# Two attention loops of a two-layer transformer kernel: handing the exponentials on in parts instead of all together

## The chip, the cores and the metric

The kernel runs on all 8 cores of one Trainium2 chip. Every core runs the same program on its own batch element (2048 tokens of width 1024), and the cores do not exchange data. The metric is the device time of one launch on the slowest core, in microseconds.

## What is computed

The reference has two layers. Layer 0 adds, to the input x, a differential attention (16 query heads, 4 key/value heads, causal, two softmaxes over half heads of 32) and a feed-forward part whose operands are quantised to FP4 in blocks of 16. Layer 1 adds a linear attention and a stack of two local-attention blocks with a GELU MLP each. The change touches the two softmax attentions only:

```python
# layer 0, differential attention: 16 heads, two score sets each, T = 2048
s1 = jnp.einsum('bhqd,bhkd->bhqk', q1, k1) * scale      # half heads, 32 wide
s2 = jnp.einsum('bhqd,bhkd->bhqk', q2, k2) * scale
a1 = jax.nn.softmax(jnp.where(causal, neg_inf, s1), axis=-1)
a2 = jax.nn.softmax(jnp.where(causal, neg_inf, s2), axis=-1)
y  = jnp.einsum('bhqk,bhkd->bhqd', a1 - lam * a2, v)     # then RMS norm, @ Wout.T

# layer 1, local attention, twice (DEPTH = 2): 8 heads of 64, window 512
sim  = jnp.einsum('bhwid,bhwjd->bhwij', bq, bk)          # each window sees itself and the one before
sim  = jnp.where(mask, -jnp.finfo(sim.dtype).max, sim)   # i < j, or i > j + 512
attn = jax.nn.softmax(sim, axis=-1)
out  = jnp.einsum('bhwij,bhwjd->bhwid', attn, bv)
```

## The kernel before

The program is written engine by engine. `te`, `ve`, `se`, `ge` and `sy` are TensorE, VectorE, ScalarE, GpSimd and SyncE, and each engine runs its own instructions in the order of the code. They meet in a few counting semaphores: `k.s_mm` is raised by TensorE, `k.s_v` by VectorE, `k.s_s` by ScalarE. `sem.inc(instr)` raises the count when that instruction is done, `sem.wait(engine)` makes an engine wait until everything raised so far in the code has arrived. `se.drain()` and `ve.drain()` wait until their engine is empty, and are often what carries the raise. The stages run one after the other, with barriers between them. PSUM is held as two tiles of four banks, `psA` and `psB`, each [128, 4, 512] in float32, and nearly all of SBUF as one tile, ARENA.

**Layer 0, `emit_l0_scores`.** For each of 8 pairs of heads (`qt`) and each of 4 blocks of 512 queries (`c`) the loop over `kt` goes through 4c+4 blocks of 128 keys. That is 8 x (4+8+12+16) = 320 iterations. In the last four of each block (`masked`) the causal diagonal runs through the tile and only columns `off` to 512 are computed, so that the width is 512, 384, 256 or 128: 128 iterations, 32 of each width. The other 192 have the width 512. One iteration:

1. TensorE makes four score tiles, `psA[:, jj]` for jj = 0 to 3, each with a bias matmul of one row (L703) and the score matmul of 32 rows (L706).
2. ScalarE waits for all four and takes four exponentials into `UT[:, jj]` (L714), then a drain, which raises `s_s` (L715).
3. If masked, VectorE multiplies the diagonal block of all four by the 0/1 mask `M01`, in one instruction of 4 x 128 columns (L720).
4. TensorE waits for that and adds four matmuls of values (V) with `UT[:, jj]` into `psB[0:65, jj]` (L729). The row 65 is the sum of the exponentials.

The next iteration's scores need `psA` to be read out (a wait on `s_s`) and stand behind the four value matmuls in TensorE's order.

**Layer 1, `emit_l1f_attn`, once for each of two blocks.** For 4 pairs of heads (`t4`), 4 windows (`w`) and 4 blocks of 128 queries (`lq`) there are 64 iterations per block, 128 in all. A query block sees `nblk` key blocks, five in 48 of the 64 iterations (640 columns), and one to four in the others. One iteration:

1. TensorE makes negated scores of both heads (jj = 0, 1), each in two banks of `psA` (L1453, L1457).
2. VectorE takes the minimum along each row, for head 0 and then head 1, into `NM` (L1466), and drains (L1467).
3. ScalarE takes both exponentials with the minima as bias into `UT[:, jj]` (L1471), and drains (L1473).
4. TensorE transposes the 2 x nblk blocks one by one through two banks of `psB` (L1483), and VectorE copies each out, those on the diagonal times a mask (L1487, L1489, L1491). From the third on, a transpose waits for the copy two before it.

After each window come the value matmuls (L1500), a few small steps and the next window.

Of the kernel before, what the change touches and what calls it, by code (L numbers as in the profile page):

```python
# [11 lines left out]
AF = mybir.ActivationFunctionType  # L12
ALU = mybir.AluOpType
AX = mybir.AxisListType
# [577 lines left out]
def emit_l0_scores(k, h, Q, K2, VT, out_h):  # L592
    nc = k.nc
    te, ve, se, ge, sy = k.te, k.ve, k.se, k.ge, k.sy
# [6 lines left out]
    UT = ar.bf(4, 512)  # L601
# [33 lines left out]
    for kt2 in range(2):  # L635
# [4 lines left out]
        for cc in range(4):  # L640
            k.s_mm.inc(te.matmul(k.psB[:, cc, :], P4t[:], SQB[:, 512 * cc:512 * cc + 512],
                                 start=True, stop=True))
# [16 lines left out]
    for kv in range(4):  # L659
        for g4 in range(4):  # L660
            off = 128 * (kv % 2) + kv // 2 + 64 * (g4 % 2)
# [6 lines left out]
    M01 = k.M01  # L668
# [3 lines left out]
    for qt in range(8):  # L672
        kvv = qt // 2
# [5 lines left out]
        for cc in range(4):  # L679
            k.s_mm.inc(te.matmul(k.psB[:, cc, :], P4t[:], SQB[:, 512 * cc:512 * cc + 512],  # L680
                                 start=True, stop=True))
# [12 lines left out]
        for c in range(4):  # L694
            nkt = 4 * c + 4
            k.s_v.wait(te)
            for kt in range(nkt):
                masked = kt >= 4 * c
                off = 128 * (kt - 4 * c) if masked else 0
                w = 512 - off  # L700
                te.wait_ge(k.s_s.h, k.s_s.n)
                for jj in range(4):
                    te.matmul(k.psA[:, jj, off:512], ones1b[32 * jj:32 * jj + 1, 0:128],  # L703
                              BT[32 * jj:32 * jj + 1, 512 * c + off:512 * c + 512],
                              start=True, stop=False, tile_position=(32 * jj, 0))
                    mm = te.matmul(k.psA[:, jj, off:512],  # L706
                                   KARR[32 * jj:32 * jj + 32, kvv, 128 * kt:128 * kt + 128],
                                   Q[32 * jj:32 * jj + 32, qt, 512 * c + off:512 * c + 512],
                                   start=False, stop=True, tile_position=(32 * jj, 0))
                    k.s_mm.inc(mm)  # L710
                k.s_mm.wait(se)
                k.s_v.wait(se)
                for jj in range(4):
                    se.activation(UT[:, jj, off:512], k.psA[:, jj, off:512], AF.Exp)  # L714
                k.s_s.inc(se.drain())  # L715
                if masked:
                    k.s_s.wait(ve)
                    uview = UT[:, :, off:off + 128]
                    m01b = M01[:].unsqueeze(1).broadcast_to((128, 4, 128))
                    k.s_v.inc(ve.tensor_tensor(uview, uview, m01b, op=ALU.mult))  # L720
                if DEV_TAP == "ut" and qt == 0 and c == 3 and kt == 0:
                    full_barrier(k)
                    dump_fm(k, UT.rearrange("p a b -> p (a b)").unsqueeze(1), k.out_h, 1)
                    return
                k.s_s.wait(te)
                if masked:
                    k.s_v.wait(te)
                for jj in range(4):
                    k.s_mm.inc(te.matmul(k.psB[0:65, jj, off:512], VT[:, kt, kvv, 0:65],  # L729
                                         UT[:, jj, off:512], start=(kt == 0), stop=(kt == nkt - 1)))  # L730
            k.s_mm.wait(ve)
            for jj in range(4):
                ve.tensor_copy(OE[0:65, jj, :], k.psB[0:65, jj, :])
# [42 lines left out]
            if DEV_TAP == "rc" and qt == 0 and c == 0:  # L776
# [8 lines left out]
                             axis=AX.X, op=ALU.add)  # L785
# [58 lines left out]
    for j in range(NT):  # L844
        k.s_st.wait(ve)
        for oc in range(2):
            pb = k.psB[:, 2 * (j % 2) + oc, :]
            te.wait_ge(k.s_v.h, max(0, k.s_v.n - 3))
            for ft in range(8):
                mm = te.matmul(pb, Q[:, ft, 128 * j:128 * j + 128],  # L850
                               WOB[:, ft, 512 * oc:512 * oc + 512],
                               start=(ft == 0), stop=(ft == 7))
# [437 lines left out]
def emit_l1f_attn(k, h, out_h, XINT, l, CQ, SQ, CK, SK,  # L1290
                  P64R, M01L, PHB, E2B, E2Q, E2K, QSR):
    te, ve, se, ge, sy = k.te, k.ve, k.se, k.ge, k.sy
    ar = k.ar
    M01 = k.M01
# [32 lines left out]
    for oc in range(12):  # L1327
        b = oc % 2
# [3 lines left out]
        for tc in range(4):  # L1332
            pb = k.psA[:, tc % 4, :]
            te.wait_ge(k.s_s.h, max(0, k.s_s.n - 3))
            for ic in range(8):
# [3 lines left out]
                               start=(ic == 0), stop=(ic == 7))  # L1339
# [13 lines left out]
    UT = ar.bf(2, 640)  # L1353
# [85 lines left out]
    NM = k.stats[:, 44:46]  # L1439
    for t4 in range(4):  # L1440
        for w in range(4):
            for lq in range(4):
                qc = 4 * w + lq
                kts = list(range(max(0, qc - 4), qc + 1))
                nblk = len(kts)
                wcols = 128 * nblk
                te.wait_ge(k.s_s.h, k.s_s.n)
                te.wait_ge(k.s_v.h, k.s_v.n)
                for jj in range(2):
                    lhs = QKVB[64 * jj:64 * jj + 64, t4, 128 * qc:128 * qc + 128]  # L1450
                    kbase = 128 * kts[0]
                    w0 = min(512, wcols)
                    mm = te.matmul(k.psA[:, 2 * jj, 0:w0], lhs,  # L1453
                                   QKVB[64 * jj:64 * jj + 64, 4 + t4, kbase:kbase + w0],
                                   start=True, stop=True, tile_position=(64 * jj, 0))
                    if wcols > 512:
                        mm = te.matmul(k.psA[:, 2 * jj + 1, 0:wcols - 512], lhs,  # L1457
                                       QKVB[64 * jj:64 * jj + 64, 4 + t4,
                                            kbase + 512:kbase + wcols],
                                       start=True, stop=True, tile_position=(64 * jj, 0))  # L1460
                    k.s_mm.inc(mm)
                k.s_mm.wait(ve)
                ve.wait_ge(k.s_s.h, k.s_s.n)
                for jj in range(2):
                    flat = k.psA[:, 2 * jj:2 * jj + 2, :].rearrange("p a b -> p (a b)")
                    ve.tensor_reduce(NM[:, jj:jj + 1], flat[:, 0:wcols], axis=AX.X, op=ALU.min)  # L1466
                k.s_v.inc(ve.drain())  # L1467
                k.s_v.wait(se)
                for jj in range(2):
                    flat = k.psA[:, 2 * jj:2 * jj + 2, :].rearrange("p a b -> p (a b)")  # L1470
                    se.activation(UT[:, jj, 0:wcols], flat[:, 0:wcols], AF.Exp,  # L1471
                                  bias=NM[:, jj:jj + 1], scale=-1.0)
                k.s_s.inc(se.drain())  # L1473
                k.s_s.wait(te)
                vb2 = k.s_v.n
                i2 = 0
                for jj in range(2):
                    for b, kt in enumerate(kts):
                        ktr = kt - 4 * w + 4
                        if i2 >= 2:  # L1480
                            te.wait_ge(k.s_v.h, vb2 + i2 - 1)
                        pvb = k.psB[:, 2 + i2 % 2, :].bitcast(BF16)[:, 0:128]
                        k.s_mm.inc(te.transpose(pvb, UT[:, jj, 128 * b:128 * b + 128], k.idb[:]))  # L1483
                        k.s_mm.wait(ve)
                        dst = UTT[:, jj, ktr, 128 * lq:128 * lq + 128]
                        if b == 0 and qc >= 4:
                            k.s_v.inc(ve.tensor_tensor(dst, pvb, M01L[:], op=ALU.mult))  # L1487
                        elif b == nblk - 1:
                            k.s_v.inc(ve.tensor_tensor(dst, pvb, M01[:], op=ALU.mult))  # L1489
                        else:  # L1490
                            k.s_v.inc(ve.tensor_copy(dst, pvb))  # L1491
                        i2 += 1
            te.wait_ge(k.s_v.h, k.s_v.n)
            ktrs = [3, 4, 0, 1, 2, 5, 6, 7] if w > 0 else [4, 5, 6, 7]
            for jj in range(2):
                for idx, ktr in enumerate(ktrs):
                    kt = ktr + 4 * w - 4
# [393 lines left out]
```

## Time and profile before

| | us |
|---|---|
| time before, median of 2 runs | 11788.0 (11786.84 to 11789.16) |
| the profiled execution's own time | 11779.26 |
| its span on the slowest core (core 6) | 11777.7 |
| spans of the eight cores | 11709.6 to 11777.7 |
| busy: TensorE, VectorE, ScalarE, GpSimd | 4204.9, 3347.4, 1550.8, 1078.3 |

No engine is busy for more than 36% of the span. The page of the profile lists what each engine did; the views that follow it are the totals by line, the timeline (each row is a start time, a duration, the engine, the line, the operation, the tiles and their shapes, and in brackets how long the engine had been idle and who released it), and sums over stretches of time. The profile's times are those of one execution.

### The profile page before, as it was taken

How to read it: one execution, taken by the hardware profiler on the slowest of the kernel's cores; microseconds unless marked ns; L12 is line 12 of the kernel's file. 1: busy time of each engine (PE TensorE's matmuls, PEld its weight loads, DVE VectorE, ACT ScalarE, POOL GpSimd, SP SyncE). 2: the span in 40 equal slices, each digit the busy share in tenths (PEclk: the TensorE clock that was granted, in tenths of full speed). 3: DMA queues.
4: the chain of work that ended last, by engine and by line, in shares of the span. 5: the costliest groups of instructions: out<-in, count | busy, mean ns of one | idle time of the engine just before them, and what ended most of it. 6: DMA issues, size and time to landing. Idle time of an engine off the chain costs nothing.

```text
span 11777.7 us, 65862 instructions; the slowest of 8 cores (11709.6 to 11777.7 us)
## 1 busy us (share of the span) xinstructions
PE 4204.9 (36%) x17922; PEld 1690.8 (14%) x18113; DVE 3347.4 (28%) x7665; ACT 1550.8 (13%) x2754; POOL 1078.3 (9%) x737
## 2 busy tenths in 40 slices
PE   0000033434444433333434233344436234244353
PEld 0000011111111111111212111111112011111111
DVE  6555542111112133233325545001003544201000
ACT  1000013333333200000111111100001111100000
POOL 1222210000000011111000000111110000111110
PEclk9999985555555667766666555677767555676666
DMA  1111110000000101111310001332331001232323
GB/s 54 34 43 43 44 28 0 1 0 0 0 0 0 62 29 47 54 31 52 93 59 10 0 1 23 34 29 22 31 36 12 0 1 22 27 29 22 36 28 70
DMA packets 563009, 326.39 MB, mean 28 GB/s; under 512 B 466694, under 2 KB 519046, under 8 KB 561628
## 3 DMA queue, kind: packets, MB, share of 16 engines
q0 software_dynamic: 406448, 125.85, 10.4%
q1 hardware_dynamic: 156212, 196.32, 5.1%
q8 instruction: 167, 2.74, 0.1%
q14 instruction: 182, 1.49, 0.0%
HBM read 388.63 MB, written 50.92 MB: 37 GB/s over the span
## 4 chain that ended last, share of the span: by engine, by line
PE 33%; DVE 20%; DMA 15%; POOL 7%; ACTq 6%; issue 6%; ACT 6%; DVEq 5%; SPq 1%; POOLq 0%; PEldq 0%
PE psA L1744 8%; DMA ARENA<-w 7%; PE psB L729 4%; ACTq L715 4%; PE psB L1772 3%; POOL qC L291 2%; POOL ARENA L317 2%; DVE qB L1399 2%; PE psA L937 2%; DMA ARENA<-wquT_s 2%; POOL ARENA L1757 2%; DMA ARENA<-x_s 2%; ACT ARENA L714 1%; PE psB L1483 1%; PE psA L940 1%
## 5 line engine op out<-in xcount | busy, mean ns | idle before, releaser
L1744 PE MATMUL psA<-ARENA 128*128 128x512 bf16 (+1 forms) x2760 | 982.1, 530 | 1624.6 <-DMA ARENA<-w 1617.0
L333 PE MATMUL psA<-c_idb,ARENA 128*128 128x128 bf16 x888 | 146.2, 257 | 2248.6 <-POOL ARENA L317 1923.0
L1778 DVE TENSOR_TENSOR ARENA<-ARENA,psB 128x512 bf16<-128x512 bf16 x64 | 41.1, 683 | 2950.2 <-PE psB L1772 2950.2
L729 PE MATMUL psB<-ARENA 128*65 128x512 bf16 (+3 forms) x1280 | 522.1, 562 | 824.5 <-ACTq L715 509.2
L714 ACT ACTIVATE ARENA<-psA 128x512 bf16<-128x512 f32 (+3 forms) x1280 | 578.8, 539 | 919.7 <-PE psA L706 919.3
L1744 PEld LDWEIGHTS psA<-ARENA 128*128 128x128 bf16 (+1 forms) x2816 | 347.8, 128 | 2259.3 <-issue 2184.5
L720 DVE TENSOR_TENSOR ARENA<-ARENA,c_m 128x512 bf16<-128x512 bf16 x128 | 54.4, 425 | 1553.0 <-ACTq L715 1553.0
L291 POOL TENSOR_TENSOR qC<-qC,qA 128x2048 f32<-128x2048 f32 (+2 forms) x70 | 284.3, 4061 | 1959.0 <-DVEq L289 1959.0
L1751 ACT ACTIVATE qC<-psA,B1GC 128x512 bf16<-128x512 f32 (+1 forms) x176 | 120.9, 687 | 2500.4 <-PE psA L1744 2500.3
L1483 PE MATMUL psB<-c_idb,ARENA 128*128 128x128 bf16 x1120 | 229.4, 270 | 564.4 <-ACTq L1473 414.3
L333 PEld LDWEIGHTS psA<-c_idb,ARENA 128*128 128x128 bf16 x888 | 91.2, 103 | 2294.4 <-issue 2272.0
L1757 POOL TENSOR_TENSOR ARENA<-qC 128x512 bf16<-128x512 bf16 (+1 forms) x176 | 201.2, 1143 | 2243.4 <-ACTq L1755 2243.4
L1772 PE MATMUL psB<-ARENA 128*128 128x512 bf16 (+1 forms) x1376 | 356.0, 412 | 3.3 <-issue 1.7
L729 PEld LDWEIGHTS psB<-ARENA 128*65 128x65 bf16 x1280 | 170.4, 161 | 1185.8 <-issue 1174.6
L937 PE MATMUL psA<-ARENA 128*128 128x512 bf16 (+1 forms) x745 | 202.1, 419 | 382.6 <-DMA ARENA<-wquT_s 268.6
L1471 ACT ACTIVATE ARENA<-psA,stats 128x640 bf16<-128x640 f32 (+4 forms) x256 | 172.1, 723 | 1048.8 <-DVEq L1467 1048.8
L317 POOL TENSOR_TENSOR ARENA<-qC,qbm 128x2048 bf16<-128x2048 bf16 (+2 forms) x70 | 230.4, 3291 | 602.5 <-DVEq L311 602.5
L947 DVE TENSOR_TENSOR ARENA<-ARENA,psA 128x512 f32<-128x512 f32 (+1 forms) x96 | 61.7, 643 | 701.3 <-ACT ARENA L944 701.3
L944 ACT ACTIVATE ARENA<-psA 128x512 f32<-128x512 f32 (+1 forms) x96 | 53.9, 561 | 1479.7 <-PE psA L940 1479.7
L293 DVE SCALAR_TENSOR_TENSOR qA<-qC,qB 128x2048 f32<-128x2048 f32 (+2 forms) x70 | 145.5, 2078 | 304.4 <-POOL qC L291 304.4
L335 DVE COPY ARENA<-psA 128x128 bf16<-128x128 bf16 x888 | 139.0, 215 | 288.2 <-PE psA L333 283.9
L275 DVE TENSOR_REDUCE qbm<-ARENA 128x128 f32<-128x2048 f32 (+2 forms) x70 | 145.1, 2073 | 255.1 <-DMA ARENA<-wu 84.7
(343 smaller groups left out, 6970.5 us busy)
## 6 DMA issues: line engine op xcount, KB each, us to landing
ARENA<-w POOLq DMA_DIRECT2D x336, 256.0 KB, 4.8
ARENA<-x_s SPq DMA_DIRECT2D x80, 512.0 KB, 3.4
x_s<-ARENA SPq DMA_DIRECT2D x48, 512.0 KB
ARENA<-wqgT_s SPq DMA_DIRECT2D x20, 1024.0 KB, 5.9
ARENA<-wquT_s SPq DMA_DIRECT2D x20, 1024.0 KB, 8.4
ARENA<-x_in SPq DMA_DIRECT2D x32, 512.0 KB, 3.7
ARENA<-wg SPq DMA_DIRECT2D x11, 1024.0 KB, 6.2
ARENA<-wu SPq DMA_DIRECT2D x11, 1024.0 KB, 6.3
```

The lines of the kernel that those rows point to most:

```text
L291: k.s_g.inc(g.tensor_tensor(C[:, 0:W], C[:, 0:W], A[:, 0:W], op=ALU.add))
L317: k.s_g.inc(g.tensor_tensor(Q3, psi3, bm12b, op=ALU.mult))
L333: k.s_mm.inc(k.te.transpose(pv, src, identity))
L714: se.activation(UT[:, jj, off:512], k.psA[:, jj, off:512], AF.Exp)
L715: k.s_s.inc(se.drain())
L729: k.s_mm.inc(te.matmul(k.psB[0:65, jj, off:512], VT[:, kt, kvv, 0:65], UT[:, jj, off:512], start=(kt == 0), stop=(kt == nkt - 1)))
L937: te.matmul(k.psA[:, 0, 0:ocw], XQF[:, ic, 128 * j:128 * j + 128], WGS[:, ic, 0:ocw], start=(ic == 0), stop=(ic == 7))
L1399: ve.reciprocal(NRM[:], NRM[:])
L1483: k.s_mm.inc(te.transpose(pvb, UT[:, jj, 128 * b:128 * b + 128], k.idb[:]))
L1744: mm = te.matmul(k.psA[0:ocw, ag, :], W1S[:, ag, b, ic, 0:ocw], XHh[:, ic, toff:toff + 512], start=(ic == 0), stop=(ic == 7))
L1757: k.s_g.inc(ge.tensor_tensor(AHq[0:ocw, hc, :], AT[0:ocw, :], GH[0:ocw, :], op=ALU.mult))
L1772: mm = te.matmul(pb, AHq[0:kcw, hc, 128 * tch:128 * tch + 128], W2R[0:kcw, hc, 512 * dc:512 * dc + 512], start=False, stop=(hc == 21))
```

## The change

In layer 0 the four exponentials are dealt with in two halves. After the second exponential `s_s` is raised by the activation itself, and not by a drain; VectorE masks these two (2 x 128 columns), TensorE does the value matmuls of these two, and then the same happens with the third and fourth. All eight instructions of ScalarE and TensorE are still there, VectorE has two smaller mask multiplications instead of one, and the one drain is gone.

In layer 1 the minimum of head 0 raises `s_v` itself, and the exponential of head 0 waits for that one only; likewise for head 1. Each exponential raises `s_s`, and the transposes of head jj wait for the exponential of head jj only (`ecnt[jj]`). Both drains are gone. No tile and no buffer changes in either loop.

```diff
--- before.py
+++ after.py
@@ -710,24 +710,27 @@
                     k.s_mm.inc(mm)
                 k.s_mm.wait(se)
                 k.s_v.wait(se)
-                for jj in range(4):
-                    se.activation(UT[:, jj, off:512], k.psA[:, jj, off:512], AF.Exp)
-                k.s_s.inc(se.drain())
-                if masked:
-                    k.s_s.wait(ve)
-                    uview = UT[:, :, off:off + 128]
-                    m01b = M01[:].unsqueeze(1).broadcast_to((128, 4, 128))
-                    k.s_v.inc(ve.tensor_tensor(uview, uview, m01b, op=ALU.mult))
+                m01b2 = M01[:].unsqueeze(1).broadcast_to((128, 2, 128))
+                for half in range(2):
+                    jjs = (0, 1) if half == 0 else (2, 3)
+                    se.activation(UT[:, jjs[0], off:512], k.psA[:, jjs[0], off:512], AF.Exp)
+                    k.s_s.inc(se.activation(UT[:, jjs[1], off:512],
+                                            k.psA[:, jjs[1], off:512], AF.Exp))
+                    if masked:
+                        k.s_s.wait(ve)
+                        uview = UT[:, jjs[0]:jjs[0] + 2, off:off + 128]
+                        k.s_v.inc(ve.tensor_tensor(uview, uview, m01b2, op=ALU.mult))
+                    k.s_s.wait(te)
+                    if masked:
+                        k.s_v.wait(te)
+                    for jj in jjs:
+                        k.s_mm.inc(te.matmul(k.psB[0:65, jj, off:512], VT[:, kt, kvv, 0:65],
+                                             UT[:, jj, off:512],
+                                             start=(kt == 0), stop=(kt == nkt - 1)))
                 if DEV_TAP == "ut" and qt == 0 and c == 3 and kt == 0:
                     full_barrier(k)
                     dump_fm(k, UT.rearrange("p a b -> p (a b)").unsqueeze(1), k.out_h, 1)
                     return
-                k.s_s.wait(te)
-                if masked:
-                    k.s_v.wait(te)
-                for jj in range(4):
-                    k.s_mm.inc(te.matmul(k.psB[0:65, jj, off:512], VT[:, kt, kvv, 0:65],
-                                         UT[:, jj, off:512], start=(kt == 0), stop=(kt == nkt - 1)))
             k.s_mm.wait(ve)
             for jj in range(4):
                 ve.tensor_copy(OE[0:65, jj, :], k.psB[0:65, jj, :])
@@ -1461,20 +1464,20 @@
                     k.s_mm.inc(mm)
                 k.s_mm.wait(ve)
                 ve.wait_ge(k.s_s.h, k.s_s.n)
+                ecnt = []
                 for jj in range(2):
                     flat = k.psA[:, 2 * jj:2 * jj + 2, :].rearrange("p a b -> p (a b)")
-                    ve.tensor_reduce(NM[:, jj:jj + 1], flat[:, 0:wcols], axis=AX.X, op=ALU.min)
-                k.s_v.inc(ve.drain())
-                k.s_v.wait(se)
-                for jj in range(2):
-                    flat = k.psA[:, 2 * jj:2 * jj + 2, :].rearrange("p a b -> p (a b)")
-                    se.activation(UT[:, jj, 0:wcols], flat[:, 0:wcols], AF.Exp,
-                                  bias=NM[:, jj:jj + 1], scale=-1.0)
-                k.s_s.inc(se.drain())
-                k.s_s.wait(te)
+                    k.s_v.inc(ve.tensor_reduce(NM[:, jj:jj + 1], flat[:, 0:wcols],
+                                               axis=AX.X, op=ALU.min))
+                    se.wait_ge(k.s_v.h, k.s_v.n)
+                    flat2 = k.psA[:, 2 * jj:2 * jj + 2, :].rearrange("p a b -> p (a b)")
+                    k.s_s.inc(se.activation(UT[:, jj, 0:wcols], flat2[:, 0:wcols], AF.Exp,
+                                            bias=NM[:, jj:jj + 1], scale=-1.0))
+                    ecnt.append(k.s_s.n)
                 vb2 = k.s_v.n
                 i2 = 0
                 for jj in range(2):
+                    te.wait_ge(k.s_s.h, ecnt[jj])
                     for b, kt in enumerate(kts):
                         ktr = kt - 4 * w + 4
                         if i2 >= 2:
```

## Rows read from the trace of the kernel before

**Rows 1.** Sums over stretches: layer 0 loop, part of it, projections, layer 1 loop.

```profile
core 6: us, PE busy (x) PEld busy (x) DVE busy (x) ACT busy (x) POOL busy (x), PEclk, DMA share, GB/s
1827.00:3990.00 2163.00, 896.89 (x4481) 277.77 (x4488) 382.28 (x1315) 713.42 (x1440) 0.00 (x0) 0.50 0.00 0
2000.00:2050.00 50.00, 27.47 (x118) 6.37 (x116) 0.00 (x0) 18.58 (x36) 0.00 (x0) 0.50 0.00 0
1650.00:1700.00 50.00, 49.74 (x228) 22.65 (x232) 0.00 (x0) 17.24 (x30) 0.00 (x0) 1.00 0.00 0
6585.00:7210.00 625.00, 240.03 (x1194) 111.42 (x1194) 259.91 (x971) 87.33 (x129) 0.00 (x0) 0.53 0.00 1
```

**Rows 2.** Timeline, layer 0, one iteration without mask.

```profile
2504.16 2.06 ACT L714 ACTIVATE ARENA<-psA 128x512 bf16<-128x512 f32 x4 [3.30 <-PE psA L706]
...
2506.39 1.89 PE L729 MATMUL psB<-ARENA 128*65 128x512 bf16 x4 [2.49 <-ACTq L715]
...
2508.21 0.62 PE L703 MATMUL psA<-ARENA,c_ones1b 1*128 1x512 bf16 x4
2509.51 2.06 ACT L714 ACTIVATE ARENA<-psA 128x512 bf16<-128x512 f32 x4 [3.30 <-PE psA L706]
```

**Rows 3.** Timeline, layer 0, the end of that iteration and the four masked widths.

```profile
2510.49 1.09 ACT L714 ACTIVATE ARENA<-psA 128x512 bf16<-128x512 f32 x2
2511.70 0.42 DVE L720 TENSOR_TENSOR ARENA<-ARENA,c_m 128x512 bf16<-128x512 bf16 x1 [47.91 <-ACTq L715]
...
2512.28 1.89 PE L729 MATMUL psB<-ARENA 128*65 128x512 bf16 x4 [3.02 <-DVE ARENA L720]
...
2515.20 1.64 ACT L714 ACTIVATE ARENA<-psA 128x384 bf16<-128x384 f32 x4 [3.62 <-PE psA L706]
...
2517.53 1.46 PE L729 MATMUL psB<-ARENA 128*65 128x384 bf16 x4 [2.59 <-DVE ARENA L720]
...
2520.08 1.21 ACT L714 ACTIVATE ARENA<-psA 128x256 bf16<-128x256 f32 x4 [3.25 <-PE psA L706]
...
2521.99 1.03 PE L729 MATMUL psB<-ARENA 128*65 128x256 bf16 x4 [2.44 <-DVE ARENA L720]
...
2523.62 0.79 ACT L714 ACTIVATE ARENA<-psA 128x128 bf16<-128x128 f32 x4 [2.33 <-PE psA L706]
...
2525.10 0.61 PE L729 MATMUL psB<-ARENA 128*65 128x128 bf16 x4 [1.74 <-DVE ARENA L720]
```

**Rows 4.** Totals by line and shape: exponentials, minima, and two rows to compare with.

```profile
L714 ACT ACTIVATE ARENA<-psA 128x512 bf16<-128x512 f32 x896 | 462.5, 603 | 634.0 <-PE psA L706 633.6
...
L1466 DVE TENSOR_REDUCE stats<-psA 128x1 f32<-128x640 f32 x192 | 149.3, 819 | 102.3 <-PE psA L1457 102.3
...
L1471 ACT ACTIVATE ARENA<-psA,stats 128x640 bf16<-128x640 f32 x192 | 141.9, 789 | 868.9 <-DVEq L1467 868.9
...
L1342 ACT ACTIVATE ARENA<-psA 128x512 bf16<-128x512 f32 x96 | 57.3, 597 | 210.6 <-PE psA L1337 210.6
...
L307 DVE TENSOR_TENSOR qC<-qC,qA 128x1024 bf16<-128x1024 bf16 x20 | 13.8, 692 | 1.5
```

**Rows 5.** Timeline, layer 1, one iteration of five key blocks.

```profile
6656.87 1.56 DVE L1466 TENSOR_REDUCE stats<-psA 128x1 f32<-128x640 f32 x2 [1.08 <-PE psA L1457]
6658.55 1.48 ACT L1471 ACTIVATE ARENA<-psA,stats 128x640 bf16<-128x640 f32 x2 [16.34 <-DVEq L1467]
...
6660.19 0.37 PE L1483 MATMUL psB<-c_idb,ARENA 128*128 128x128 bf16 x2 [3.51 <-ACTq L1473]
6660.56 0.23 DVE L1487 TENSOR_TENSOR ARENA<-psB,M01L 128x128 bf16<-128x128 bf16 x1 [2.14 <-PE psB L1483]
6660.70 0.21 DVE L1491 COPY ARENA<-psB 128x128 bf16<-128x128 bf16 x1
6660.90 0.23 PEld L1483 LDWEIGHTS psB<-c_idb,ARENA 128*128 128x128 bf16 x2 [0.60 <-issue]
...
6661.65 0.24 PEld L1483 LDWEIGHTS psB<-c_idb,ARENA 128*128 128x128 bf16 x2 [0.51 <-issue]
```

## Prediction

> **What bounds the kernel now.** I read the sums over stretches first. Layer 0's attention loop takes 2163 us, and in it TensorE is busy for 897 us, ScalarE for 713 and VectorE for 382, with no DMA traffic at all [rows 1]. The loop of layer 1 takes 625 us for one of its two blocks, with 240, 87 and 260 us [rows 1]. No engine is full in either: they take turns. So I went to the timeline, where the reader is to see that each engine's work begins just after the end of another's.
>
> An iteration of layer 0 without mask: four exponentials from 2504.16 to 2506.22, 0.17 us later four value matmuls at 2506.39, scores at 2508.21, the next exponentials at 2509.51, and so 5.35 us in all. While ScalarE works TensorE is idle ("2.49 <-ACTq L715"), and while TensorE works ScalarE is ("3.30 <-PE psA L706") [rows 2]. With a mask 0.12 us of handing over, 0.42 us of VectorE and 0.16 us of handing over come between the exponentials and the value matmuls [rows 3].
>
> An iteration of layer 1 with five key blocks: two minima from 6656.87 to 6658.43, 0.12 us later two exponentials to 6660.03, 0.16 us later the first transpose. From there on transposes and copies go in pairs at 0.75 us a pair (6660.90 to 6661.65) [rows 5].
>
> Everything that one of these chains loses comes off the span one to one, as the stages are serial and no DMA waits in them.
>
> **Layer 0, no mask (192 iterations).** The second exponential ends 1.09 us after the first began, the fourth 2.06 us [rows 3, 2]. After the change value matmuls 0 and 1 can start 0.17 us after the end of the second, while ScalarE goes on. What does a value matmul cost in a stream? The totals of four fall by 0.43 us for every 128 columns less (1.89, 1.46, 1.03, 0.61 [rows 3]), which is 0.107 us per matmul and 128 columns: 0.43, 0.32, 0.21 and 0.11 us for the four widths. Likewise the exponentials: 2.06, 1.64, 1.21, 0.79 fall by 0.42 per 128 columns for four, and the third one starts 0.98 us after the first (2509.51 to 2510.49), so 0.49 each at 512 columns [rows 2, 3]. Two matmuls take 0.86 us, exponentials 2 and 3 take 0.97 us: the first half of the matmuls is hidden with 0.1 us to spare. Matmuls 2 and 3 then begin where all four begin today, and the next scores come 2 x 0.43 = 0.86 us earlier. 192 x 0.86 = **165 us**. Cover gone, this is zero.
>
> **Layer 0, mask (128 iterations, 32 of each width).** Two matmuls fewer on the path: 2 x (0.43 + 0.32 + 0.21 + 0.11) = 2.14 us, times 32 = 68 us. They are hidden here too, since at each width two exponentials take longer than two matmuls (at 128 columns 2 x 0.17 against 2 x 0.11). And the mask is cut in two, of which only the second is on the path. No row shows 2 x 128 columns. 512 columns took 0.42 us, 1024 in the same types 0.69 us [rows 3, 4]: 0.27 per 512, so 0.16 fixed, and 0.29 us for 256. That is 0.13 x 128 = 17 us gained. At worst the half costs as much as the whole, and the gain is 0. Sum with mask **85 us**.
>
> The fixed part is where a rule speaks against the change. The Trainium skill (VectorE: DVE Perf Modes, section on the TRN2 errata) says that each VectorE instruction on SBUF pays a fixed price between instructions, so that small tiles pay it again and again. By its figures (58 cycles and one for every two columns, at 0.96 GHz) the half would be an estimated 0.19 us and the whole 0.33, where the trace has 0.42; the difference of 0.13 us is the same, and so is the sum. The doubled fixed part lies beside the other half's exponentials.
>
> **Layer 1 (128 iterations).** Today the first transpose comes 3.32 us after the first minimum began. After: minimum 0 (0.82 us [rows 4]) + 0.12 + exponential 0 (0.79 [rows 4]) + 0.16 = 1.89 us, so 1.43 us earlier. Is anything late next? Minimum 1 ends 1.56 us after the start, +0.12 exponential 1 may begin at 1.73, when ScalarE is free, and ends at about 2.5; +0.16, head 1 can be transposed from 2.7. Head 0's five transposes last until 1.89 + 5 x 0.375 = 3.8, so this wait is covered. 96 iterations have 640 columns: 96 x 1.43 = 137 us. The other 32 have 128 to 512, half as many on average, and I scale the gain by columns: 32 x 0.72 = 23 us. **160 us** in both blocks.
>
> **The waits as such.** Raising a semaphore in mid-stream must be quick, and must not part instructions that overlap. For VectorE the trace shows both: the copy of 6660.56 ends at 6660.79, TensorE goes on at 6660.90 while the next copy, begun at 6660.70, still runs [rows 5]. For ScalarE there is no such row. Bounds: nothing, or each iteration loses the overlap of consecutive exponentials, 0.60 - 0.49 = 0.11 us [rows 4], once: 320 x 0.11 = 36 us. I take nothing, for the likeness to VectorE's row. The drains that go may give a little back: behind a drain TensorE came 0.17 us after ScalarE's last work, behind VectorE's raise 0.11 us (6660.79 to 6660.90 [rows 5], the weight load, with the matmul 0.03 us after it). 448 hand-overs x 0.03 = 13 us: not counted, but in the range.
>
> **Sum.** 165 + 85 + 160 = 410 us off. On the profiled execution's own 11779.3 this is 11369; it stands 9 us below the median of the runs, 11788.0, which gives **11378 us**, 3.5% faster.
>
> **Rivals.**
>
> *Handed on late.* ScalarE's raise from the second exponential shows only when its queue is empty. Then layer 0's halves give nothing, and layer 1's, where ScalarE has one exponential at a time between waits, stay: 11788 - 160 = 11628 us, within 2%. For it: no row of ScalarE. Against it: VectorE's row above.
>
> *The clock rises.* In the loop of layer 0 TensorE has its granted clock at 0.50, the level of 1.2 GHz, throughout, though it is busy for 27.5 of 50 us in a stretch without breaks; in the projections, busy for 49.7 of 50, it has 1.00, 2.4 GHz [rows 1]. After the change it is busy for the same time in iterations of 4.5 instead of 5.35 us. If that lifts it, two value matmuls (0.86) and the scores up to the exponentials (1.30 us, 2508.21 to 2509.51 [rows 2]) halve at best: 1.08 us x 192 + 0.67 x 128 = 293 us more, 11085 us. Against it: the dense part of an iteration, value matmuls and scores with 0.1 us between, is there today and does not lift it, and the change breaks this part rather than lengthens it. The Trainium skill (TensorE: Matmul & The Clock Gate, Part 1) has the clock throttled until sustained activity releases it; by this rule a denser loop comes nearer to release, and this rival is what that would give.
>
> *Slower: streams that hinder each other.* Today ScalarE's reads of `psA` never meet matmuls or minima in these loops; after, two exponentials per iteration run beside value matmuls, and layer 1's beside a minimum or transposes. Overlapped time of exponentials: 192 x 0.97 + 128 x 0.61 (mean width) = 264, and 96 x 0.79 + 32 x 0.5 = 92 us, 356 in all. They would have to become 2.15 times as long for the 410 us to be gone (410 / 356), and 2.8 times to be 2% slower; at three times it is 11378 + 712 = 12090 us. Against it: in the projections, where ScalarE reads one bank while TensorE fills the next without pause, the same shape took 597 ns, against 603 here [rows 1, 4].
>
> **Chances.** As computed, with sizes off by little: 0.88. Late: 0.06. Clock: 0.04. Hindered: 0.02, half of it beyond 2% slower. The range takes the bounds of the first case: 11378 - 13 - 20 for the scaled part of layer 1 and the hand-overs there is 11345; with the mask's half at full price (17), the lost overlap (36) and 20 for the scaled part it is 11451, and I reach to 11470 for the state of the clock in the stages behind, which begin at another moment. About 2% is what a measurement of this kernel can tell from no change: faster by over 2% (under 11552 us) 0.93, within 2% 0.06, slower 0.01.
>
> **What would show it.** The loop of layer 0 should last 1913 us instead of 2163, those of layer 1 545 instead of 625. In the timeline of an iteration without mask there should be two pairs of value matmuls, the first beside exponentials, and 4.5 us from one iteration to the next. The first transpose of layer 1 should stand 1.9 us behind the first minimum, with a second wait of TensorE of near zero. Half a mask should take 0.29 us, exponentials 0.60. The prediction is wrong if the first pair of matmuls starts only after the fourth exponential, if exponentials beside matmuls last longer, or if the granted clock of the loop is not 0.50.

## The result and the profile after

The changed kernel takes 11357.18 us (median of 11 runs, 11328.51 to 11424.57), where the kernel before takes 11796.55 us on the same chips (median of 10 runs, 11738.04 to 11868.69). The ratio is 0.9633, with a 95% interval of 0.9606 to 0.9659: 402 to 465 us, or 3.4% to 3.9%, less. The profiled execution took 11322.74 us.

The two loops can be read apart from the rest in each trace, from the start of a loop's first score matmul to the end of its last transpose (in layer 0 the last of L809, in layer 1 the last of L1534, counted in lines of the kernel before). Lowest to highest of the eight cores, in us:

| kernel | layer 0's loop | layer 1, first block | layer 1, second block | all the rest |
|---|---|---|---|---|
| before | 2176.2 to 2176.4 | 625.2 to 628.6 | 626.0 to 626.5 | 8281.7 to 8348.4 |
| after | 1921.0 to 1921.4 | 545.5 to 547.9 | 546.9 to 548.9 | 8257.6 to 8304.3 |
| forecast | 1926 (2176 - 250) | 547 (627 - 80) | 546 | as before |

The loops lost 255, 80 and 78 us, 413 us in all (means of the eight cores), where 410 us were forecast. The rest differs by 67 us (before) and 47 us (after) from core to core in one and the same execution. The cores that are longer there had a lower granted TensorE clock in some stage outside the loops; in the kernel before, for one, the stretch behind the last loop took 1843.6 us on core 6 at a mean granted clock of 0.66, and 1787.6 us on core 1 at 0.70. What the total lost beyond the 413 us, 26 us, is smaller than these differences. So the loops are the better instrument here: they agree within 1 us (layer 0) or 4 us (layer 1) between the cores.

Sums over stretches of the kernel after, as in [rows 1]; columns are the busy times of the engines, TensorE's granted clock, the DMA share and GB/s:

```profile
core 6: us, PE busy (x) PEld busy (x) DVE busy (x) ACT busy (x) POOL busy (x), PEclk, DMA share, GB/s
1824.00:3750.00 1926.00, 938.56 (x4501) 230.75 (x4508) 410.43 (x1480) 715.55 (x1443) 0.89 (x1) 0.50 0.00 1
...
6326.00:6880.00 554.00, 252.92 (x1200) 112.90 (x1200) 271.73 (x980) 89.60 (x129) 0.75 (x1) 0.54 0.00 1
```

ScalarE's busy time in layer 0's loop is that of before, 716 against 713 us, in 237 us less. Nothing became cheaper; two things happen at once. In layer 0's loop the granted clock is still 0.50, its lower level of 1.2 GHz; in layer 1's loop it is 0.54 in the mean, where it was 0.53.

The timeline of one iteration without mask, kernel after, to be held against [rows 2]:

```profile
2485.20 0.60 ACT L716 ACTIVATE ARENA<-psA 128x512 bf16<-128x512 f32 x1 [2.42 <-PE psA L706]
2485.69 0.59 ACT L717 ACTIVATE ARENA<-psA 128x512 bf16<-128x512 f32 x1
2486.17 0.61 ACT L716 ACTIVATE ARENA<-psA 128x512 bf16<-128x512 f32 x1
...
2486.43 2.02 PE L727 MATMUL psB<-ARENA 128*65 128x512 bf16 x4 [1.49 <-ACT ARENA L717]
2486.64 0.62 ACT L717 ACTIVATE ARENA<-psA 128x512 bf16<-128x512 f32 x1
...
2488.38 0.62 PE L703 MATMUL psA<-ARENA,c_ones1b 1*128 1x512 bf16 x4
...
2489.68 0.60 ACT L716 ACTIVATE ARENA<-psA 128x512 bf16<-128x512 f32 x1 [2.42 <-PE psA L706]
```

The value matmuls (L727) begin at 2486.43, 0.15 us after the second exponential has ended at 2486.28 (2485.69 + 0.59), while the third runs. The next scores stand 1.12 us behind the fourth's end (2487.26 to 2488.38), where it was 1.99 us (2506.22 to 2508.21 [rows 2]). From one iteration to the next it is 4.48 us instead of 5.35.

One iteration of layer 1 with five key blocks, kernel after, against [rows 5]; the last line is the next iteration's first minimum:

```profile
6392.95 1.55 DVE L1470 TENSOR_REDUCE stats<-psA 128x1 f32<-128x640 f32 x2 [1.08 <-PE psA L1460]
6393.87 1.52 ACT L1474 ACTIVATE ARENA<-psA,stats 128x640 bf16<-128x640 f32 x2 [15.74 <-DVE stats L1470]
...
6394.81 0.37 PE L1486 MATMUL psB<-c_idb,ARENA 128*128 128x128 bf16 x2 [2.04 <-ACT ARENA L1474]
...
6399.67 0.82 DVE L1470 TENSOR_REDUCE stats<-psA 128x1 f32<-128x640 f32 x1 [1.05 <-PE psA L1460]
```

ScalarE starts 0.92 us after the first minimum has begun (before, 1.68), and the transposes after 1.86 us (before, 3.32). The next iteration's minimum comes 6.72 us after this one's; before it was 8.10 us, from 6656.87 [rows 5] to this line of the kernel before:

```profile
6664.97 1.56 DVE L1466 TENSOR_REDUCE stats<-psA 128x1 f32<-128x640 f32 x2 [1.05 <-PE psA L1457]
```

Totals by line of the kernel after: count, busy time and mean in ns, idle time before and who ended it, to compare with [rows 4]:

```profile
L717 ACT ACTIVATE ARENA<-psA 128x512 bf16<-128x512 f32 x448 | 271.0, 605 | 0.0
L716 ACT ACTIVATE ARENA<-psA 128x512 bf16<-128x512 f32 x448 | 269.4, 601 | 466.2 <-PE psA L706 465.9
L1470 DVE TENSOR_REDUCE stats<-psA 128x1 f32<-128x640 f32 x192 | 149.3, 819 | 102.0 <-PE psA L1460 102.0
L1474 ACT ACTIVATE ARENA<-psA,stats 128x640 bf16<-128x640 f32 x192 | 146.3, 793 | 732.0 <-DVE stats L1470 732.0
L722 DVE TENSOR_TENSOR ARENA<-ARENA,c_m 128x256 bf16<-128x256 bf16 x256 | 74.7, 292 | 1284.4 <-ACT ARENA L717 1282.8
```

Each of L716 and L717 mixes exponentials that run beside matmuls with others that do not, so the rows of the trace have to be taken by their place in the iteration. Of the four exponentials of 512 columns (core 6), the third and fourth, which now run beside value matmuls, take 606 and 618 ns in the mean; before, with TensorE idle, they took 605 and 618. The second minimum, now beside an exponential, takes 814 ns as before. The exponentials of 640 columns take 794 ns for head 0, beside a minimum (before 793), and 793 for head 1, beside transposes (before 786). Half a mask takes 292 ns.

### The profile page after: what moved, and what is told of

Its sections match the earlier page's. It is cut to its first block, busy times and chain, and to the rows that moved or that the text cites. A ratio compares the mean times of both kernels' runs of the same rounds, so it can differ in the third digit from the quotient of the medians.

```text
span 11321.2 us, 66246 instructions; the slowest of 8 cores (11274.5 to 11321.2 us)
## 1 busy us (share of the span) xinstructions
PE 4235.2 (37%) x17922; PEld 1634.8 (14%) x18113; DVE 3385.5 (30%) x7793; ACT 1555.4 (14%) x2754; POOL 1078.3 (10%) x737
## 4 chain that ended last, share of the span: by engine, by line
PE 34%; DVE 21%; DMA 16%; POOL 8%; ACT 7%; issue 6%; DVEq 5%; ACTq 2%; SPq 1%; POOLq 0%; PEldq 0%
PE psA L1747 9%; DMA ARENA<-w 8%; PE psB L727 5%; PE psB L1775 3%; POOL qC L291 3%; POOL ARENA L317 2%; DVE qB L1402 2%; DMA ARENA<-x_s 2%; PE psA L940 2%; DMA ARENA<-wquT_s 2%; POOL ARENA L1760 2%; ACT ARENA L716 2%; PE psB L1486 2%; PE psA L1340 1%; PE psA L943 1%
## 5 line engine op out<-in xcount | busy, mean ns | idle before, releaser
L727 PE MATMUL psB<-ARENA 128*65 128x512 bf16 (+3 forms) x1280 | 563.1, 557 | 528.4 <-ACT ARENA L717 327.1
L722 DVE TENSOR_TENSOR ARENA<-ARENA,c_m 128x256 bf16<-128x256 bf16 x256 | 74.7, 292 | 1284.4 <-ACT ARENA L717 1282.8
L716 ACT ACTIVATE ARENA<-psA 128x512 bf16<-128x512 f32 (+3 forms) x640 | 343.9, 537 | 676.3 <-PE psA L706 676.0
L1486 PE MATMUL psB<-c_idb,ARENA 128*128 128x128 bf16 x1120 | 253.8, 270 | 378.7 <-ACT ARENA L1474 245.3
L717 ACT ACTIVATE ARENA<-psA 128x512 bf16<-128x512 f32 (+3 forms) x640 | 346.2, 541 | 0.0
L1775 PE MATMUL psB<-ARENA 128*128 128x512 bf16 (+1 forms) x1376 | 333.0, 392 | 3.1 <-issue 1.8
L727 PEld LDWEIGHTS psB<-ARENA 128*65 128x65 bf16 x1280 | 121.4, 144 | 980.3 <-issue 977.8
```

The costliest lines, as they stand in the source:

```text
L716: se.activation(UT[:, jjs[0], off:512], k.psA[:, jjs[0], off:512], AF.Exp)
L717: k.s_s.inc(se.activation(UT[:, jjs[1], off:512], k.psA[:, jjs[1], off:512], AF.Exp))
L1775: mm = te.matmul(pb, AHq[0:kcw, hc, 128 * tch:128 * tch + 128], W2R[0:kcw, hc, 512 * dc:512 * dc + 512], start=False, stop=(hc == 21))
```

## The experiments

All of them are told by the length of the loops, on all eight cores as above, and by the total where it was timed four times. Ratios are to the kernel before on the same chip. The other three were timed once, and one time tells less than the loops: 11635.72 us for `l0_unsplit_nodrain`, 11635.26 for `l0_late`, 11515.39 for `l1_min_apart`. Edits are against the changed kernel where nothing else is said, and shortened where `...` stands.

### Each part alone

`l0_only` has layer 0's loop as changed and layer 1's as before; `l1_only` the other way round. Each takes one of the two hunks of the diff above.

> Only layer 0's loop is changed, layer 1's is that of before. If the two parts act apart and each only by what it takes off its own chain, layer 0's loop lasts about 1921 us (2176 before, by the first score matmul and the last transpose of the loop), layer 1's loops 626 us as before, and the time falls by about 255 us. If the gain of the whole were in part one of clock or DMA in other stages, the sum of the two single changes would miss that of both.

> Only layer 1's loop is changed. Own chain: each of the two loops 547 us instead of 626, layer 0's loop 2176 as before, and the time about 158 us lower. Rival (a minimum and an exponential that read PSUM at the same time hinder each other): exponentials and minima longer than 789 and 819 ns, gain under 158.

| | layer 0's loop | layer 1's loops | time (4 runs) | ratio |
|---|---|---|---|---|
| l0_only | 1921.3 to 1922.3 | 625.3 to 628.8 | 11540.48 | 0.9796 (0.9754 to 0.9838) |
| l1_only | 2176.5 to 2178.5 | 546.5 to 548.8 | 11609.41 | 0.9869 (0.9827 to 0.9911) |

Each part shortens its own loop by what it does together with the other and leaves the other's loop alone. Both totals are as expected (255 us is a ratio of 0.978, 158 us one of 0.987). In the loops the gain is the sum of two independent ones; the totals agree with that, but their intervals of about 50 us to either side could not show it alone.

### Is it the drain?

In `l0_unsplit_nodrain` the four exponentials of layer 0 are handed on together as before; only the drain is replaced by a raise on the fourth. Layer 1 is as in the change.

```diff
-                for jj in range(4):
-                    se.activation(UT[:, jj, off:512], k.psA[:, jj, off:512], AF.Exp)
-                k.s_s.inc(se.drain())
+                for jj in range(4):
+                    ex = se.activation(UT[:, jj, off:512], k.psA[:, jj, off:512], AF.Exp)
+                k.s_s.inc(ex)
```

(The lines with a minus are those of the kernel before.)

> Layer 0's loop as before, with four exponentials handed on together, but the raise sits on the fourth exponential and the drain is gone; layer 1 as in the change. If the drain was only a carrier of the raise, each hand-over is 0.03 us shorter (0.14 instead of 0.17) and the loop lasts about 2166 us (before 2176, changed 1921). If the drains were the cost and not the order, it lasts near 1921 us.

The loop lasts 2169.7 to 2170.8 us: 6 us less than before, of 255. From its timeline:

```profile
2506.49 2.07 ACT L714 ACTIVATE ARENA<-psA 128x512 bf16<-128x512 f32 x4 [3.27 <-PE psA L706]
...
2508.71 1.89 PE L729 MATMUL psB<-ARENA 128*65 128x512 bf16 x4 [2.47 <-ACT ARENA L714]
```

TensorE now starts 0.15 us after the exponentials end (2508.56), not 0.17. The drain cost 0.02 us per iteration; it was no more than the place where the raise sat.

### Is it the first pair of matmuls beside exponentials?

`l0_late` raises, splits and masks in halves as the change does, but TensorE waits for both halves.

```diff
-                    k.s_s.wait(te)
-                    if masked:
-                        k.s_v.wait(te)
-                    for jj in jjs:
-                        k.s_mm.inc(te.matmul(...))
+                k.s_s.wait(te)
+                if masked:
+                    k.s_v.wait(te)
+                for jj in range(4):
+                    k.s_mm.inc(te.matmul(...))
```

> The change, but in layer 0 TensorE waits for both halves of exponentials (and masks) before its four value matmuls; everything of ScalarE and VectorE is as in the change. If the gain of layer 0 lies in the first two value matmuls beside exponentials 2 and 3, nearly all of it goes: left are the 6 us of the drain (loop 2170) and 0.13 x 128 = 17 us of the mask, so the loop lasts about 2153 us. If the raises and smaller masks were the gain, it lasts 1921 us as in the change.

The loop lasts 2153.9 to 2154.9 us. Its timeline shows the four matmuls behind the fourth exponential again:

```profile
2423.30 0.62 ACT L717 ACTIVATE ARENA<-psA 128x512 bf16<-128x512 f32 x1
...
2424.07 1.89 PE L727 MATMUL psB<-ARENA 128*65 128x512 bf16 x4 [2.47 <-ACT ARENA L717]
```

So of layer 0's 255 us, 6 are the drain, 16 the smaller mask (2170 less 2154; 17 were worked out), and 233 the pair of matmuls that runs beside exponentials (2154 less 1921; 165 + 68 = 233 were worked out).

### What a finer hand-over brings, and what a raise costs

`l0_quarters` hands the exponentials of layer 0 on one by one.

```diff
-                for half in range(2):
-                    jjs = (0, 1) if half == 0 else (2, 3)
-                    se.activation(UT[:, jjs[0], off:512], k.psA[:, jjs[0], off:512], AF.Exp)
-                    k.s_s.inc(se.activation(UT[:, jjs[1], off:512],
-                                            k.psA[:, jjs[1], off:512], AF.Exp))
+                for jq in range(4):
+                    jjs = (jq,)
+                    k.s_s.inc(se.activation(UT[:, jq, off:512], k.psA[:, jq, off:512], AF.Exp))
...
-                        uview = UT[:, jjs[0]:jjs[0] + 2, off:off + 128]
-                        k.s_v.inc(ve.tensor_tensor(uview, uview, m01b2, op=ALU.mult))
+                        uview = UT[:, jq, off:off + 128]
+                        k.s_v.inc(ve.tensor_tensor(uview, uview, M01[:], op=ALU.mult))
```

> The change, with layer 0's exponentials handed on one by one instead of two by two, each with its own mask and its own value matmul. If the chain only holds what is not yet handed on, one value matmul less is on it: 192 x 0.43 + 128 x 0.27 = 117 us, and a quarter of the mask (about 0.23 us) instead of a half (0.29) gives 8 more, so layer 0's loop lasts about 1797 us instead of 1921. If each raise in mid-stream costs ScalarE the overlap of 0.11 us with the next exponential, two more raises per iteration cost 320 x 2 x 0.11 = 70 us and the loop lasts about 1867 us. If the first matmuls really start no earlier than today's change has them, no change.

The loop lasts 1804.6 to 1805.4 us, 117 less than with halves where 125 were expected, and the time is 11266.17 us (4 runs), a ratio of 0.9581 (0.9548 to 0.9614). An iteration without mask, from its timeline:

```profile
2375.64 2.06 ACT L715 ACTIVATE ARENA<-psA 128x512 bf16<-128x512 f32 x4 [2.00 <-PE psA L706]
...
2376.38 2.08 PE L724 MATMUL psB<-ARENA 128*65 128x512 bf16 x4 [1.00 <-ACT ARENA L715]
...
2379.70 2.06 ACT L715 ACTIVATE ARENA<-psA 128x512 bf16<-128x512 f32 x4 [2.00 <-PE psA L706]
```

The four exponentials take 2.06 us, with a raise on each, as they did with a single drain behind all four [rows 2]: raises in mid-stream cost ScalarE none of its overlap. An iteration takes 4.06 us, 0.42 us less than with halves, one value matmul. That is 82 us in the 192 iterations without mask, and the masked ones of 512, 384 and 256 columns gave 37 us, as worked out. The 8 us that are missing lie in the last iteration of each block, the one of 128 columns:

```profile
2406.37 0.79 ACT L715 ACTIVATE ARENA<-psA 128x128 bf16<-128x128 f32 x4 [1.62 <-PE psA L706]
2406.75 0.73 DVE L719 TENSOR_TENSOR ARENA<-ARENA,c_m 128x128 bf16<-128x128 bf16 x4 [1.62 <-ACT ARENA L715]
2407.12 0.98 PE L724 MATMUL psB<-ARENA 128*65 128x128 bf16 x4 [1.01 <-ACT ARENA L715]
```

The four value matmuls, each behind waits of its own, take 0.98 us, where four in one go took 0.61 [rows 3]. From the first exponential to VectorE's first copy of the result it is 1.89 us in the mean of the 32 such iterations (core 6), against 1.83 in the change, where 0.17 us less were worked out: 32 x 0.23 = 7 us. With so few columns a finer hand-over gains nothing.

### Layer 1: one hand-over without the other

In `l1_min_apart` the minima hand on one by one, but head 0's transposes wait for both exponentials.

```diff
-                    te.wait_ge(k.s_s.h, ecnt[jj])
+                    te.wait_ge(k.s_s.h, ecnt[1])
```

> The change, but in layer 1 the transposes of head 0 wait for both exponentials; the minima still hand on one by one. Own chain: exponential 1 ends 1.68 + 0.79 = 2.47 us after the first minimum began, first transpose at 2.61 instead of 1.87 us, so 0.74 us x 48 and less for the short ones per block: each loop about 587 us (change 547, before 626). The two hand-overs are then worth half each.

The loops last 586.8 to 588.7 and 589.0 to 591.1 us. From the timeline:

```profile
6457.55 1.55 DVE L1470 TENSOR_REDUCE stats<-psA 128x1 f32<-128x640 f32 x2 [1.08 <-PE psA L1460]
6458.47 1.52 ACT L1474 ACTIVATE ARENA<-psA,stats 128x640 bf16<-128x640 f32 x2 [16.02 <-DVE stats L1470]
6460.14 0.37 PE L1486 MATMUL psB<-c_idb,ARENA 128*128 128x128 bf16 x2 [2.77 <-ACT ARENA L1474]
```

The first transpose stands 2.59 us behind the first minimum, between 3.32 before and 1.86 after, and 40 of the 80 us of the first block and 36 of the 78 of the second are left (means of the cores). Each of the two hand-overs is worth about one half.

### Taking the rest of TensorE's work off the chain, and the clock

The change leaves two value matmuls and the scores on layer 0's chain. In `l0_ahead` TensorE makes the next iteration's scores between the two halves of value matmuls; ScalarE's second half waits, by the count of `s_mm`, for the second pair of value matmuls of the iteration before, which read what it overwrites. The loop's core in short, with words in place of code where `...` stands:

```diff
-            for kt in range(nkt):
-                ... scores of kt ...
+            nscore = scores(0)
+            for kt in range(nkt):
                 for half in range(2):
+                    se.wait_ge(k.s_mm.h, nscore if half == 0 else max(nscore, npv))
                     ... two exponentials, mask ...
+                    if half == 1 and kt + 1 < nkt:
+                        nscore = scores(kt + 1)
                     ... two value matmuls ...
+                npv = k.s_mm.n
```

> The change, and in layer 0 TensorE makes the next iteration's scores between the two halves of value matmuls, as soon as the four exponentials have read psA. No value matmul is on the chain then: exponentials 2.06 + 0.14 + scores 1.30 = 3.5 us per iteration instead of 4.49. 192 x 0.99 = 190 us, and for the masked widths 512, 384, 256 (1.38 + 1.18 + 0.96) x 32 = 113 us: loop about 1618 us, time about 303 us lower than the change. Rival (clock): TensorE is then busy for about 0.8 of the time; if its granted clock rises from 0.50 to 1.00 in the loop, the scores halve too (0.65 us less at best, 3.5 to 2.85) and the loop falls to about 1450 us.

The loop lasts 1644.3 to 1645.3 us, 276 less than the change, and the time is 11080.14 us (4 runs), a ratio of 0.9417 (0.9360 to 0.9473). An iteration without mask takes 3.44 us, and the scores (L701) now come first:

```profile
2606.74 0.62 PE L701 MATMUL psA<-ARENA,c_ones1b 1*128 1x512 bf16 x4
...
2607.72 1.06 PE L738 MATMUL psB<-ARENA 128*65 128x512 bf16 x2
2607.98 0.60 ACT L724 ACTIVATE ARENA<-psA 128x512 bf16<-128x512 f32 x1 [1.38 <-PE psA L704]
...
2611.42 0.60 ACT L724 ACTIVATE ARENA<-psA 128x512 bf16<-128x512 f32 x1 [1.38 <-PE psA L704]
```

The loop is 27 us longer than expected, and the masked iterations show why. In one of 384 columns, whose exponentials end at 2300.39 (2299.90 + 0.49):

```profile
2298.36 1.06 PE L738 MATMUL psB<-ARENA 128*65 128x512 bf16 x2
...
2299.51 0.49 ACT L724 ACTIVATE ARENA<-psA 128x384 bf16<-128x384 f32 x1
2299.60 0.29 DVE L731 TENSOR_TENSOR ARENA<-ARENA,c_m 128x256 bf16<-128x256 bf16 x1 [2.15 <-ACT ARENA L725]
2299.90 0.49 ACT L725 ACTIVATE ARENA<-psA 128x384 bf16<-128x384 f32 x1
...
2300.04 0.82 PE L738 MATMUL psB<-ARENA 128*65 128x384 bf16 x2 [0.62 <-DVE ARENA L731]
...
2300.80 0.41 PE L701 MATMUL psA<-ARENA,c_ones1b 1*128 1x256 bf16 x4
```

The next scores start 0.41 us after the exponentials, not 0.14: they stand in TensorE's order behind the first pair of value matmuls, and that pair waits for its mask until 2299.89 and for 0.15 us more. The expectation had left this wait out. It had also left out the third exponential's wait: it starts at 2299.51, 0.09 us after the second pair of value matmuls of the iteration before has ended (2298.36 + 1.06), and the four exponentials take 1.76 us in the mean at this width instead of 1.64. In means of core 6, the 96 masked iterations that scores follow are 0.34 us longer than expected (33 us) and the 32 last ones 0.12 us longer than in the change (4 us), while the 192 without mask take 3.45 us, 0.05 less than the 3.50 expected (9 us): together 28 us more.

The clock is the other point of this run. In a stretch of it without breaks:

```profile
2600.00:2650.00 50.00, 35.69 (x162) 7.91 (x154) 10.70 (x39) 23.17 (x49) 0.00 (x0) 0.50 0.00 1
```

TensorE is busy for 35.7 of 50 us, against 27.5 in the kernel before [rows 1], and its granted clock is 0.50 as it was. In this loop that much more activity does not lift it. What would is not shown by these runs, and the busy share of a stretch alone does not tell. The projections, with 49.7 of 50 us at 1.00 [rows 1], came after stretches that stood at 1.00 already with little to do, and elsewhere 30 busy us went with a mean clock of 0.80 (kernel before):

```profile
1500.00:1550.00 50.00, 3.00 (x22) 2.28 (x22) 26.82 (x40) 0.00 (x0) 11.04 (x2) 1.00 0.15 43
4450.00:4500.00 50.00, 30.36 (x125) 13.27 (x129) 10.73 (x23) 0.00 (x0) 6.06 (x4) 0.80 0.22 53
```

`both_ahead` does the same in layer 1: the scores of the next query block are made after the second exponential, between the transposes of head 0 and of head 1.

```diff
                 for jj in range(2):
                     te.wait_ge(k.s_s.h, ecnt[jj])
+                    if jj == 1 and lq < 3:
+                        nsc = scores1(lq + 1)
                     for b, kt in enumerate(kts):
```

> As the one before, and in layer 1 the scores of the next query block are made between the transposes of head 0 and of head 1. The scores (1.06 us from the last copy to the first minimum) leave the chain, but stand in the middle of the transposes for about 0.54 us: 0.5 us x 36 per block less, each loop about 525 us instead of 547. If the stop in the transposes costs as much as the scores did, 547 us stays.

Layer 1's loops last 532.6 to 534.6 us, 14 less than in the change where 22 were expected; layer 0's is that of the run before. The time is 11037.83 us (4 runs), a ratio of 0.9362 (0.9324 to 0.9400), and so this is the fastest kernel of the study, though its interval overlaps with that of `l0_ahead`. From the timeline:

```profile
6389.82 0.27 PE L1501 MATMUL psB<-c_idb,ARENA 128*128 128x128 bf16 x1 [0.34 <-DVE ARENA L1509]
6390.05 0.61 PE L1462 MATMUL psA<-ARENA 64*128 64x512 bf16 x2
...
6390.70 0.40 PE L1501 MATMUL psB<-c_idb,ARENA 128*128 128x128 bf16 x2
```

Between head 0's last transpose and head 1's first there are 0.88 us, where the change has 0.25 in the mean (core 6). The first transpose also stands 1.97 us behind the first minimum instead of 1.86. Of the 1.06 us of scores that were taken off the chain, some 0.7 came back at these two places: an iteration takes 6.38 us, 0.34 less than in the change.

## Why the prediction was right

- **What bounds these loops.** That the engines take turns, and that a gain in them comes off the span one to one, held: single changes moved their own loop and not the other.
- **Layer 0 without mask, 165 us, and the masked matmuls, 68 us.** The experiment that undoes just the early start of the first pair loses 233 us, their sum. The step that two matmuls take 0.86 us and are covered by 0.97 us of exponentials is seen in the timeline: the second pair's weights are loaded at 2487.38, 0.12 us after the end of the fourth exponential (2486.64 + 0.62), and so it starts where it would have without the first.
- **The mask, 17 us.** The half took 292 ns where 0.29 us were worked out from the rows of 512 and 1024 columns, and the part gave 16 us. The duration of 0.19 us that the prediction estimated from the figures of the Trainium skill (VectorE: DVE Perf Modes, section on the TRN2 errata) is not what the trace shows; the trace decides, and the fixed part is 0.16 us. This part is paid twice, as that section of the Trainium skill says of small tiles, but only once on the chain.
- **Layer 1, 160 us.** Measured 158, and here two small errors cancel. The first transpose came after 1.86 us, forecast 1.89; over both blocks (core 6) the first transposes stand 168 us earlier, 141 us in the iterations of 640 columns (137 forecast) and 28 in the shorter ones (23 forecast, by scaling). Of this 7 us were lost again between the first transpose and the work that follows the last; some 4 us more I did not follow up. The place of the loss is seen: from head 0's last transpose to head 1's first it takes 0.25 us in the mean instead of 0.17, and there stands the new wait of TensorE, for a count long reached. It is not the overlap that costs this: `l1_min_apart`, where both exponentials have ended before the first transpose, has the same 0.25 us. The wait by itself was not tested.
- **The waits as such.** Taken at nothing, with bounds of 36 us lost and 13 us gained. Raises in mid-stream cost ScalarE nothing: four exponentials with a raise on each take 2.06 us. The drain gave back 6 us in layer 0, and layer 1 lost about as much behind the first transposes.
- **The sum.** 410 us forecast, 413 measured in the loops; that it is as close as 3 us is in part luck, as the errors of layer 1's terms show. The median fell by 439 us. The 26 us beyond the loops are less than what the other stages differ by between cores of one execution, and no run ties them to the change: the mean of these stages over the cores is 8312 us before and 8284 after, but also 8310 in `l0_only` and 8331 in `l1_min_apart`. The forecast of 11378 us stands 21 us above the measured median of 11357.
- **The rivals.** *Handed on late* fell by the timeline, where matmuls start 0.15 us after the second exponential. *Hindered* fell by the durations: taken by their place, what now overlaps grew by at most 7 ns, and these 7 ns (head 1's exponential of 640 columns) are there in `l1_min_apart` too, before any transpose has begun. *The clock rises* fell in the changed kernel and again in `l0_ahead`, at more activity than the change brings. The Trainium skill's rule in the prediction (TensorE: Matmul & The Clock Gate, Part 1), that sustained activity releases the clock, is neither borne out nor contradicted by this: no run raised the clock of layer 0's loop.

## What to carry to other kernels

Where engines take turns on one chain, count per iteration what each waits for, and hand work on in parts: the gain is the part of the consumer's work that then lies under the producer's, here two matmuls of 0.43 us under two exponentials of 0.97 us, and it can be forecast to a few us from differences between rows of several widths. A drain that only carries a semaphore costs little (0.02 us in layer 0's loop); what costs is that it stands behind all of the work. Parts can be too small: at 128 columns handing on one by one gained nothing. After that, look for what else on the chain needs only a buffer that is already free: moving the next scores forward gave more (276 us) than the change's own part in layer 0 (255 us), but in the masked iterations they inherited the wait of what stood ahead of them in the same engine's order.

## What the runs showed of the hardware that was not expected

ScalarE's reads of one half of PSUM (`psA`) while TensorE writes the other (`psB`), and while VectorE reads other banks, left the durations as they were: 606 and 618 ns against 605 and 618 for the third and fourth exponential of 512 columns, 794 against 793 for head 0's of 640 beside a minimum, 814 both times for the second minimum. TensorE stayed at a granted clock of 0.50 in a stretch of 50 us in which it was busy for 71% of the time (`l0_ahead`). And the step from head 0's last transpose to head 1's first, with a wait for a count long reached between them, took 0.25 us in the changed kernel, in `l1_only` and in `l1_min_apart`, against 0.16 to 0.17 in the kernel before and in `l0_only`, which lack that wait.
